# Where in SBUF the two operands of each TensorE product begin: a decoder layer in split fp32r products

## What is computed

```python
x = layernorm(x + attention(x, W_Q, W_K, W_V, W_out, b_out))      # causal, 16 heads of 64, 8 key/value groups
x = layernorm(x + cross_attention(x, ctx, ln_w, ln_b, Wq, Wkv, Wout, mask, 5))   # 8 heads of 64, 5 of 77 rows
x = layernorm(x + ffn(x, w_gate, w_up, w_down))                   # silu(gate) * up, hidden width 768
```

## Time and profile before

| | us |
|---|---|
| three runs, median (lowest to highest) | 2037.97 (2037.02 to 2039.48) |
| the profiled execution | 2038.91 |
| its span, first to last instruction | 2037.1 |

### The profile page before, as it was taken

One profiled execution on the slowest core, in us unless ns is written; L12 is line 12 of the kernel. 1 busy time (PEld: TensorE's weight loads), 2 busy tenths in 40 slices (PEclk: granted clock), 3 DMA queues, 4 the chain that ended last, 5 costly groups with the idle time before them and its releaser, 6 DMA issues.

```text
span 2037.1 us, 50598 instructions
## 1 busy us (share of the span) xinstructions
PE 2008.3 (99%) x18176; PEld 1845.4 (91%) x18176; DVE 1545.8 (76%) x5708; ACT 1322.5 (65%) x3992; POOL 375.3 (18%) x624
## 2 busy tenths in 40 slices
PE   8999999999999999999999999999999999999997
PEld 7899999999999999999999999999999999999886
DVE  6877777777777777777777777777777777777764
ACT  8866666667666666666666666666666666666642
POOL 3112111211211111112121112112121211121121
PEclk9999999999999999999999999999999999999998
DMA  5100000000000000000000000000000000000000
GB/s 163 32 8 22 18 22 12 11 19 19 22 12 19 11 19 22 18 12 22 8 21 19 12 22 8 22 18 22 12 19 11 19 22 19 12 11 19 13 7 11
DMA packets 49606, 41.19 MB, mean 20 GB/s; under 512 B 19536, under 2 KB 47568, under 8 KB 49360
## 3 DMA queue, kind: packets, MB, share of 16 engines
q1 hardware_dynamic: 49360, 37.96, 6.4%
HBM read 29.56 MB, written 8.39 MB: 19 GB/s over the span
## 4 chain that ended last, share of the span: by engine, by line
PE 95%; DVE 1%; ACT 1%; DMA 1%; issue 1%; POOL 0%; SPq 0%; POOLq 0%; DVEq 0%; ACTq 0%
PE gen L441 20%; PE gen L442 19%; PE gen L443 19%; PE s_ps L581 9%; PE z_ps L623 7%; PE gen L529 3%; PE pt_ps L602 3%; PE gen L538 3%; PE gen L542 3%; PE pt_ps L603 3%; PE pt_ps L607 3%; PE z_ps L625 3%; PE gen L509 2%; PE gen L500 1%; PE gen L553 1%
## 5 line engine op out<-in xcount | busy, mean ns | idle before, releaser
L954 ACT ACTIVATE SM<-SM,least 128x128 f32<-128x128 f32 (+1 forms) x1024 | 452.2, 447 | 35.2 <-DVE least L1479 35.1
L884 ACT ACTIVATE PT<-pt_ps 128x512 f32<-128x512 f32 (+1 forms) x512 | 237.5, 485 | 239.7 <-PE pt_ps L603 237.4
L1479 DVE CUSTOM_DVE_ANT_0 SM<-s_ps,causal 128x128 f32<-128x128 f32 (+1 forms) x1024 | 314.7, 352 | 19.2 <-PE s_ps L581 14.3
L1492 DVE TENSOR_SCALAR SM<-SM,total 128x128 f32<-128x128 f32 (+1 forms) x1024 | 282.3, 339 | 9.0
L1858 POOL TENSOR_TENSOR H_lo<-gated,H_hi 128x256 fp32r<-128x256 f32 x192 | 141.7, 745 | 517.6 <-ACT H_hi L884 517.5
L937 ACT ACTIVATE gated<-gen 128x256 f32<-128x256 f32 x192 | 73.6, 383 | 202.6 <-PE gen L443 202.5
L581 PE MATMUL s_ps<-KT,QT 64*128 64x128 f32 (+1 forms) x2048 | 201.5, 336 | 1.4 <-ACT KT L884 0.7
L954 ACT ACTIVATION_READ_ACCUMULATOR SM<-SM,least 128x1 f32 x1024 | 196.1, 192 | 0.0
L1456 DVE SCALAR_TENSOR_TENSOR gated<-gated,gen 128x256 f32<-128x256 f32 x192 | 80.9, 421 | 120.5 <-ACT gated L937 120.1
L623 PE MATMUL z_ps<-PT,Vt 128*64 128x256 f32 x1024 | 168.1, 399 | 0.0
L581 PEld LDWEIGHTS s_ps<-KT,QT 64*128 64x128 f32 x2048 | 147.7, 187 | 21.7 <-issue 6.4
(11 more groups left out here) (185 smaller groups left out, 6507.8 us busy)
## 6 DMA issues: line engine op xcount, KB each, us to landing
xT_in<-in_xT SPq DMA_DIRECT2D x32, 256.0 KB, 2.9
x_in<-in_x SPq DMA_DIRECT2D x32, 256.0 KB, 2.8
out<-rows SPq DMA_DIRECT2D x32, 256.0 KB, 2.2
ctx_in<-in_ctxT SPq DMA_DIRECT2D x32, 77.0 KB, 2.8
mask_in<-in_maskT SPq DMA_DIRECT2D x32, 77.0 KB, 2.6
SX<-in_wq SPq DMA_DIRECT2D x1, 512.0 KB, 6.3
rows<-in_wv SPq DMA_DIRECT2D x1, 512.0 KB, 7.4
xwk<-in_xwkv SPq DMA_DIRECT2D x1, 512.0 KB, 8.1
```

What stands on the lines that cost most here:

```text
L884: return act.activation(o, i, ACT.Copy)
L954: ins = act.activation(part, part, ACT.Exp, scale=-1.0, bias=least[:, i % 4, n:n + 1], accum_out=total[:, i % 4, n:n + 1])
L1479: ins = dve.tensor_tensor_reduce(SM[:, i % 4, at:at + keys], s_ps[bank][:, col:col + keys], causal[:, S - keys:S], -SCALE, -3 * NEG, ALU.a ...
L1492: ins = dve.tensor_scalar(part, part, total[:, i % 4, n:n + 1], None, ALU.mult)
```

## The change

Only the order of the declarations in SBUF is changed. Names, shapes, instructions, their order, waits and transfers are the same. The total size is the same (227264 bytes).

```diff
--- before.py
+++ after.py
@@ -184,19 +184,28 @@
         def halves(name, shape):
             return sb(name + "_hi", shape, F32R), sb(name + "_lo", shape, F32R)
 
+
+
+
         wq_s = halves("wq", [P, KD, HE])
         wk_s = halves("wk", [P, KD, KE])
-        wv_s = halves("wv", [P, KD, KE])
-        wo_s = halves("wo", [P, NP, D])
         xwq_s = halves("xwq", [P, KD, XE])
-        xwk = sb("xwk", [P, KD, XE])
-        xwv_s = halves("xwv", [P, KD, XE])
-        xwo_s = halves("xwo", [P, XP, D])
         wg_s = halves("wg", [P, KD, HID])
         wu_s = halves("wu", [P, KD, HID])
+        den = sb("den", [P, T, 2, XH])
+        wv_s = halves("wv", [P, KD, KE])
+        xwv_s = halves("xwv", [P, KD, XE])
+        least = sb("least", [P, 4, 4])
+        wo_s = halves("wo", [P, NP, D])
+        xwo_s = halves("xwo", [P, XP, D])
         wd_s = halves("wd", [P, KH, D])
-
-
+        xT_s = halves("xTs", [P, KD, S])
+        NX_s = halves("NX", [P, KD, S])
+        NT_s = halves("NT", [P, KD, S])
+        total = sb("total", [P, 4, 4])
+        Z_s = halves("Z", [P, NP, S])
+        H_s = halves("H", [P, KH, S])
+        xwk = sb("xwk", [P, KD, XE])
         lnw = sb("lnw", [P, KD])
         lnb = sb("lnb", [P, KD])
         bias = sb("bias", [P, D])
@@ -205,15 +214,11 @@
 
         x_in = sb("x_in", [P, T, D])
         xT_in = sb("xT_in", [P, KD, S])
-        xT_s = halves("xTs", [P, KD, S])
         QT = sb("QT", [P, 2, 2, S])
         KT = sb("KT", [P, NJ, S])
         Vt = sb("Vt", [P, T, KE])
         SM = sb("SM", [P, 4, PAIR])
-        least = sb("least", [P, 4, 4])
-        total = sb("total", [P, 4, 4])
         PT = sb("PT", [P, 2, PAIR])
-        Z_s = halves("Z", [P, NP, S])
 
         rows = sb("rows", [P, 2 * T * D])
         X = rows[:, 0:T * D].rearrange("p (t d) -> p t d", t=T)
@@ -223,9 +228,6 @@
         X2 = gated[:, 2 * S:2 * S + T * D].rearrange("p (t d) -> p t d", t=T)
         XN_t = XN[:, :].rearrange("p (t d) -> p t d", t=T)
         Y = XN_t
-        NX_s = halves("NX", [P, KD, S])
-        NT_s = halves("NT", [P, KD, S])
-        H_s = halves("H", [P, KH, S])
         ones = sb("ones", [P, 1])
         minus_half = sb("minus_half", [P, T])
         eps = sb("eps", [P, T])
@@ -244,7 +246,6 @@
         VX = sb("VX", [P, XE])
         SX = sb("SX", [P, T, XH, V])
         pmax = sb("pmax", [P, T, 3, XH])
-        den = sb("den", [P, T, 2, XH])
         QX = sb("QX", [P, XH * P])
         QP = sb("QP", [P, XH * P])
 
```

## The result

The changed kernel takes **2031.54 us** (median of 6 runs, 2030.12 to 2033.14) against 2038.45 (6 runs, 2037.02 to 2039.81) of the kernel before: a ratio of 0.9967, 95% interval 0.9957 to 0.9976. That is 6.9 us less. The forecast was 2022.0; its direction held, its size did not: less than half of the gain came. The profiled execution took 2031.16 us, with a span of 2029.4.

The account below looks back on a forecast made before the run. TensorE, busy 2008.3 of 2037.1 us, was taken as the bound. 37 triples turning fast give 15.7 us off the profiled 2038.9, so 2023.2; the median lies 0.9 lower, 2022.3, forecast as 2022.0, range 2004 to 2042.

Parts of the forecast that it names:

- What bounds the kernel: TensorE, busy 2008.3 of 2037.1 us; time taken from each split matmul comes off nearly one for one.
- Placement as a cause: Split products' two paces, 0.340 and 0.353 us a triple, depend in part on loaded minus streamed start address.
- Rival 2: Pace is set by when a run's first load starts, not by address: 2038, within 3 us; chance 0.17.
- That -64 never settles and 64 does: At -64 (Q, K, OUT, XOUT, DOWN) no slow run turns fast by itself; at +64 (FFN, XQ) some do.
- The seams: FFN to OUT, OUT to FFN, Q to FFN, K to DOWN become +64: free themselves, they decide whether a pace is handed on.
- the count: Two thirds of stretches go fast, from FFN's and XQ's 13 of 20: 31 of 92 triples slow instead of 68.
- the term of 15.7 us: Gain from 37 more fast triples a turn: 37 x 13.3 ns x 32.
- Rival 1: With +64 inside and across seams every stretch goes fast: gain 28.9 us less 1 to 2, 2010; chance 0.26.
- Rival 3: FFN0, OUT and FFN3 lose their fast entry, the slow pace spreads over OUT and FFN: 10.2 us more, 2048; chance 0.15.
- Rival 4: Split products drop below 113.3 ns to the transposes' 108 ns: 44 us on top of full gain, 1966; chance 0.03.
- V and the plain products: V fills and plain float32 work: nothing taken; bounds 3.4 us either way for V, 2 us for plain work.

Follow-up runs that it names:

- the six uniform distances: Changed kernel with one distance for every split product but XV and every seam but V to FFN: -64, 0, 128, 32, 80, 96; 2044.10 to 2058.89 us.
- the mixed placement: Changed kernel with Q and K alone put back to distance -64, the rest left: 2023.56 us, ratio 0.9926 to the kernel before.

## Why the prediction was half right

- **What bounds the kernel:** right. The time followed TensorE's pace nearly one for one, from 2023.6 to 2058.9 us over these kernels.
- **Placement as a cause:** right, and shown by the six uniform distances. Rival 2 (placement not the cause) falls. The rule that bears on it, that of the Trainium skill's page "SBUF — State Buffer", section "Who interferes with whom", by which the two read ports are independent and TensorE never waits on anyone, does not agree with these runs: the distance between the two starts moves the matmul's pace from 113.3 to 120.0 ns. Its "never waits" may hold against other engines; for a stream and its own loads these paces speak against it, though no run looks at the ports themselves. Even so, rival 2's observation, both paces at one address, was true and was the part that I gave too little weight.
- **That -64 never settles and 64 does:** right (none of 232 long stretches at -64 settled; 93 of 231 at 64 did).
- **The seams:** right in kind and size. OUT to FFN1 is worth 3.4 us of pace. K0 hands its pace to DOWN, as the step said, but had it to give in only three of the steady turns, each of which shows DOWN short.
- **The step that failed is the count**, "13 of 20, about two thirds", applied to all 92 triples. It came to 61 short triples in a turn; the runs showed 40 on average (36 and half of XOUT). The mechanism was there and the term of 15.7 us should have been 6.8. The 20 stretches were from the beginning and the end of the run and one odd turn, where each entry is another draw. The steady turn repeats the same entries some 28 times, so that one bad entry counts 28 times: K1, Q1 and Q2, Q3, FFN5 and both XQ were long in all of them, not in a third. The earlier trace rows had shown XQ1 long at 64 in a steady turn, as the prediction says; it blamed the seam of -64 behind Q3 (it lies between Q3 and FFN5, which runs before XQ1), and with that seam at 64, XQ1 stayed long behind a long Q3 and FFN5. The right sample was the steady turn's own four entries at distance 64: FFN0 and FFN3 short, FFN4 and XQ0 long; a half, each kept in turn after turn.
- **What was safe** was the seam: FFN1 and FFN2 behind OUT, 8 triples or 3.4 us. The other 60 long triples hung on six entries: K1 (with Q1 and Q2, 12), Q3 (with FFN5 and XQ1, 12), Q0 (with K0 and DOWN, 20), XOUT (8), FFN4 and XQ0 (4 each). Each is a lot of 1.7 to 8.5 us, all of it or nothing. What came was FFN4's, half of XOUT's, and Q0's in three turns.
- **Rival 1** (the rule throughout) falls with the same step: it needs all six entries to be good, which 0.26 was too much for. **Rival 3** did not come: FFN0 settled as before and OUT had its pace. **Rival 4** did not come: no stretch of any of the kernels ran below 113.3 ns. V and the plain products cost nothing (V's excess 2.35 before, 2.18 after), and the waits of the earlier trace rows stayed at 2.7 us each.
- The range, 2004 to 2042, held the time.

**Open:** why a distance of 64 settles and -64 doesn't, and what in the moment of entry selects the pace. XOUT in the kernel after is short in two turns and long in the next two, with its addresses and its program unchanged, so that something beyond the turn's own program takes part. No run separates it.

## What to carry to other kernels

Where every matmul of a stream has a load of its own, look at the time from start to start: two nearly equal levels at one shape may mean, as they did here, that the start addresses of what is streamed and what is loaded are worth a sweep over their distance modulo 256 bytes, for each product, and for the seams between products. Judge it by the steady turn and by whole-kernel timing, not by stretches from the ends of a run: a repeated loop repeats one entry's luck as often as it turns. And a uniform rule need not be best: the mixed placement gave twice the gain of the uniform one.

## What the runs showed of the hardware that I had not expected

- The pace of a 128x256 product over a 128x128 load goes by the distance between the starts of its two operands in SBUF: 120.0 ns at 0 (in OUT; the mean is 119.6), 113.3 or 117.7 at 64 and -64, and at 32, 80, 96 and 128 cycles of unequal intervals with means of 118.0 to 119.2 ns (OUT at 96: 116, 119, 122, 120, 116 and again). With 512 columns the order is another one: 228.6 ns at 0, 233.3 at 64. Placement alone moved this kernel by 35 us, 1.7%.
- The two levels at 64 and -64 are states, kept over dozens of products and over seams of the same distance: OUT's 48 matmuls ran at 113.3 ns in each of 29 turns.
- One extra transpose of 109 ns ahead of a stretch turned a pace in all 29 steady turns in one place (XQ0), in 13 in another (K1 to Q2, always behind a long XOUT), and in none in a third (Q3).
